# Two 8-expert mixtures: who scales and who adds the two expert outputs of every token at the end

## The chip, the cores and the metric

One core of a Trainium2 chip. The metric is the device time of one execution in microseconds (us), the median of several. Engines are named as in the profile: PE (TensorE), DVE (VectorE), ACT (ScalarE), POOL (GpSimd), SP (SyncE, which issues most DMAs).

## What is computed

2048 tokens of 128 values, in fp32, go through six stages, each with a residual: f0 (a 64-expert mixture), a0 (attention), g0 (the 64-expert mixture again), f1 (an 8-expert mixture), a1 (attention), g1 (the 8-expert mixture again). The change touches f1 and g1:

```python
probs = softmax(x @ Wg + bg)                       # x is layer-normed, 8 experts
h = relu(einsum('bsd,edf->bsef', x, W1) + b1)
all_out = einsum('bsef,efd->bsed', h, W2) + b2
top_vals, top_idx = top_k(probs, 2)
weights = top_vals / (sum(top_vals) + 1e-9)
out = sum(selected(all_out, top_idx) * weights)    # two outputs per token
x = x + 0.5 * out
```

## The kernel before, in words

`mixture_one` (L746) is built twice, as f1 and as g1. Tokens lie as 16 tiles of 128 in `core.x` (128 partitions, 16 tiles, 128 values). Every token's row is sent by GpSimd's indirect DMAs to the region of each of its two experts in DRAM, 39 tiles of 128 slots come back, and PE puts each through its expert. The outputs `y` go by an indirect DMA each (L902, `DMA_INDIRECT`, 39 of them, the last work of GpSimd in the stage) to `back_dram`, which is in the order of the tokens again.

The end of the stage, which the change rewrites, is this. SP waits until all 39 indirect DMAs have landed and reads `back_dram` into `back` (128 partitions, 16 tiles, K = 2 outputs, 128 values) in four quarters of four tiles each (L872, 512 KB a quarter, semaphores `back_loaded[q]`). Meanwhile DVE works out `weight` (L1211 to L1221), the factor of each output of each token, with the 0.5 in it. What is left is x += weight0 * back0 + weight1 * back1:

- Quarters 0 and 1: DVE alone, 8 instructions of 128x128 a quarter (L1228, `scalar_tensor_tensor`, multiply and add in one).
- Quarters 2 and 3: ACT scales both outputs in place, 8 instructions of 128x128 a quarter (L1039), and DVE adds them, 2 instructions of 128x512 a quarter (L1236).

The loop of DVE and the loop of ACT run over the quarters in order. `x_final` counts finished quarters. In g1, SP stores a quarter to the output when it is final (L877), and the program ends when the four stores have landed. In f1, nothing reads `x_final`; every engine drains and meets the others at `stage_end` (L3092), and then a1 starts, with DVE's layer norm of x (L675).

Three other places give rows for the prediction. In a0, GpSimd multiplies and adds tiles of 128x512 (L2063, L2067), and DVE subtracts 128x32 values, both operands in SBUF, by the helper `rest_part` (L732). In f0, GpSimd subtracts 128x512 by the same helper (L732), and DVE makes 128x1024 blocks with `tensor_scalar` from SBUF to SBUF (L1847, L1870). At the end of each stage GpSimd's queue has a drain (L3092).

Of the kernel before, what the change touches and what calls it, by code (L numbers as in the profile page):

```python
# [18 lines left out]
ALU = mybir.AluOpType  # L19
ACT = mybir.ActivationFunctionType  # L20
# [36 lines left out]
class Core:  # L57
# [11 lines left out]
    def sem(self, name):  # L69

        s = self.sem_ctx.enter_context(self.nc.semaphore(name))
        self.stage_sems.append(s)
        return s
# [12 lines left out]
class Front:  # L86


    K, ROW, REGION = 2, 132, TOKENS
# [656 lines left out]
def mixture_one(core, name, ctx, w):  # L746
# [9 lines left out]
    K = Front.K  # L756
# [37 lines left out]
    weight = sb("weight", [P, K, TILES])  # L794
# [9 lines left out]
    back = sb("back", [P, TILES, K, P])  # L804
# [4 lines left out]
    sem = lambda n: core.sem(f"{name}_{n}")  # L809
# [12 lines left out]
    fr.expect([wave_sent[v] for v, n in enumerate(halves_in) for _ in range(n)])  # L822
    w_loaded = sem("w_loaded")
    copied = sem("copied")
    back_scaled = sem("back_scaled")
    weight_ready = sem("weight_ready")
    x_loaded = [sem(f"x_loaded{i}") for i in range(len(GROUPS))]
# [7 lines left out]
    x_final = sem("x_final")  # L835
# [43 lines left out]
    def gpsimd(pool):  # L879
        if early:  # L880
            early.gpsimd(pool)
        fr.fill(pool)
        for g in range(fr.groups):
            fr.number(pool, g)
        pool.memset(lower[:, :, :], 1.0).then_inc(lower_filled, 1)
        pool.iota(fill[:, :], [[SLOTS, FULL]], base=0, channel_multiplier=0,
                  allow_small_or_imprecise_dtypes=True).then_inc(lower_ready, 1)
        pool.iota(tile_number[:, :], [[1, PASSES]], base=0, channel_multiplier=0,
                  allow_small_or_imprecise_dtypes=True).then_inc(lower_ready, 1)
        pool.memset(taken[:, E1:E1 + 1], 0.0).then_inc(lower_ready, 1)  # L890
        pool.wait_ge(lower_filled, 1)
        pool.affine_select(out=lower[:, :, :], in_=lower[:, :, :], compare_op=ALU.is_gt, fill=0.0,
                           base=0, pattern=[[1, E1], [-1, E1]], channel_multiplier=0).then_inc(lower_ready, 1)
        fr.fills.wait(pool)
        pool.wait_ge(fr.numbered, 2 * fr.groups)
        for g in range(fr.groups):
            pool.wait_ge(fr.slots_ready, g + 1)
            pool.wait_ge(fr.rows_doubled, g + 1)
            fr.scatter(pool, g)
        for i in range(PASSES):  # L900
            pool.wait_ge(y_ready, i + 1)
            pool.indirect_dma_start(back_dram[:, :],  # L902
                                    bass.IndirectOffsetOnAxis(ap=xin[:, i, P:P + 1].bitcast(I32), axis=0),
                                    y[i % YBUF][:, :], None, bounds_check=K * TOKENS - 1,
                                    oob_is_err=False).then_inc(y_sent[i % YBUF][0], 16)

    def tensor(pe):
        def turned(g):
# [85 lines left out]
    def scalar(act):  # L994
        def take(g):
            act.wait_ge(fr.turned, g + 1)
            if g:
                act.wait_ge(fr.logits_done, g)
            act.activation(fr.xnT[:, :], bank[g], ACT.Copy).then_inc(fr.xnT_ready, 1)

        fr.deviation(act, 0)
        take(0)
        fr.double(act, 0)
        fr.deviation(act, 1)
        take(1)
        fr.double(act, 1)
        for g in (2, 3):
            fr.normalise_by_shift(act, g)
            take(g)
            fr.double(act, g)  # L1010

        def xT_out(i):
            act.wait_ge(x_turned, i + 1)
            if i >= 2:
                act.wait_ge(h_done, i - 1)
            act.activation(xT[:, i % 2, :], bank[6 + i % 2][:, 0:SLOTS], ACT.Copy).then_inc(xT_ready, 1)  # L1016

        xT_out(0)
        xT_out(1)
        for i in range(PASSES):  # L1020
            if i >= 2:
                act.wait_ge(y_done, i - 1)
            act.wait_ge(h_done, i + 1)
            for c in range(FC1):
                act.activation(hT[:, i % 2, c, :], bank[i % 2][:, P * c:P * c + P], ACT.Relu,  # L1025
                               bias=wt[i % WBUF][:, B1 + c:B1 + c + 1]).then_inc(relu_done, 1)
            if i + 2 < PASSES:
                xT_out(i + 2)
            if early and 0 <= i - HIGH_AT < len(early.cuts):
                early.high(act, i - HIGH_AT)  # L1030
        act.wait_ge(shifted, 1)
        act.activation(ex[:, :, :], ex[:, :, :], ACT.Exp).then_inc(exp_done, 1)

        act.wait_ge(weight_ready, 1)
        for q in (2, 3):
            act.wait_ge(back_loaded[q], 16)
            for k in range(K):
                for t in range(4 * q, 4 * q + 4):
                    act.activation(back[:, t, k, :], back[:, t, k, :], ACT.Copy,  # L1039
                                   scale=weight[:, k, t:t + 1]).then_inc(back_scaled, 1)  # L1040

    def vector(dve):
        c_ = Chain(chain)

        def step(ins):
            dve.wait_ge(c_.sem, c_.on(ins))
# [174 lines left out]
            step(dve.tensor_reduce(weight[:, k, :], part[:, :, :], AX.X, ALU.add))  # L1221
        dve.sem_inc(weight_ready, 1)

        for q in range(2):
            dve.wait_ge(back_loaded[q], 16)
            for k in range(K):
                for t in range(4 * q, 4 * q + 4):
                    last = dve.scalar_tensor_tensor(core.x[:, t, :], back[:, t, k, :], weight[:, k, t:t + 1],  # L1228
                                                    core.x[:, t, :], ALU.mult, ALU.add)
                step(last)  # L1230
            dve.sem_inc(x_final, 1)
        for q in (2, 3):
            for k in range(K):
                dve.wait_ge(back_scaled, 4 * (K * (q - 2) + k + 1))
                xq = core.x[:, 4 * q:4 * q + 4, :]
                step(dve.tensor_tensor(xq, xq, back[:, 4 * q:4 * q + 4, k, :], ALU.add))  # L1236
            dve.sem_inc(x_final, 1)

    return dict(sync=sync, gpsimd=gpsimd, tensor=tensor, scalar=scalar, vector=vector)


# [1813 lines left out]
def build(nc, w, out, stages):  # L3055
# [87 lines left out]
STAGES = [  # L3143
    ("f0", mixture_zero), ("a0", attention_zero), ("g0", mixture_zero),
    ("f1", mixture_one), ("a1", attention_one), ("g1", mixture_one),
]

# [45 lines left out]
```

## Time and profile before

| what | us |
|---|---|
| runs | 993.63, 1002.97, 995.65 |
| median | 995.65 |
| the profiled execution | 1004.14 |
| its span | 1002.4 |
| busy: PE, DVE, ACT, POOL | 852.5, 721.0, 547.9, 299.4 |

The profiled execution's own time is 1.7 us longer than its span, and 8.5 us longer than the median. Busy time is that of all instructions of an engine. L12 is line 12 of the kernel. A duration is the time from an instruction's start to its end; consecutive instructions of DVE and ACT overlap a little, so a group's duration is shorter than the sum over its members. An entry in square brackets is the idle time ahead of an instruction and what ended it.

### The profile page before, as it was taken

The numbers are of one execution on the slowest core, as the hardware profiler recorded it, in microseconds if no ns is written. First come the engines' busy times: TensorE is split into PE (matmuls) and PEld (weight loads), VectorE is DVE, ScalarE is ACT, GpSimd is POOL, SyncE is SP. The second block draws the span as 40 slices with busy tenths as digits, with TensorE's granted clock in tenths as the row PEclk, the third lists the DMA queues.
The fourth block names the chain that finished last, engine by engine and source line by source line (L and its number), as shares of the span: only waits on it lengthen the run. The fifth ranks groups of instructions, "written<-read, shape, count | busy, mean of one in ns | idle before, by whom it ended". The sixth has DMA issues, their size and how long they took to land.

```text
span 1002.4 us, 23097 instructions
## 1 busy us (share of the span) xinstructions
PE 852.5 (85%) x7244; PEld 637.4 (64%) x7244; DVE 721.0 (72%) x2591; ACT 547.9 (55%) x1498; POOL 299.4 (30%) x423
## 2 busy tenths in 40 slices
PE   5899987899995899975999188999999998659992
PEld 4457854466553457754899165677767766548992
DVE  7757888457765866886867658877787788478665
ACT  4232043467775413113568338877887888435663
POOL 2033124743301001305777280001000000057772
PEclk9999996579998799995999679999999999959996
DMA  9208951111303503116362246544646462073314
GB/s 250 64 0 295 387 191 44 44 44 45 89 4 88 159 1 101 42 30 196 86 181 64 91 147 190 169 148 133 184 132 185 127 191 86 10 213 92 106 46 132
DMA packets 135459, 120.00 MB, mean 120 GB/s; under 512 B 11011, under 2 KB 115739, under 8 KB 135348
## 3 DMA queue, kind: packets, MB, share of 16 engines
q1 hardware_dynamic: 130804, 110.09, 36.6%
q0 software_dynamic: 4544, 8.54, 2.5%
q8 instruction: 56, 0.92, 0.4%
q14 instruction: 55, 0.45, 0.1%
HBM read 67.45 MB, written 51.80 MB: 119 GB/s over the span
## 4 chain that ended last, share of the span: by engine, by line
PE 60%; DVE 14%; ACT 13%; issue 5%; SPq 3%; DMA 3%; DVEq 1%; POOL 0%; POOLq 0%; ACTq 0%
PE psum L1613 6%; PE psum L1527 5%; PE psum L967 4%; PE psum L976 4%; PE psum L2277 4%; PE psum L2825 3%; ACT a_L L2955 3%; PE psum L2205 3%; ACT a_L L2953 3%; PE psum L2874 3%; PE psum L2861 2%; PE psum L741 2%; PE psum L1553 2%; ACT a_PT L2964 2%; PE psum L2169 2%
## 5 line engine op out<-in xcount | busy, mean ns | idle before, releaser
L2459 DVE TENSOR_REDUCE a_negmax<-psum 128x2 f32<-128x512 f32 x128 | 83.0, 686 | 43.4 <-PE psum L2205 40.3
L2405 ACT ACTIVATE a_PT<-psum 128x1024 f32<-128x1024 f32 x64 | 64.9, 1020 | 14.7 <-PE psum L2214 14.3
L2955 ACT ACTIVATE a_L<-a_L,a_least 128x256 f32<-128x256 f32 x128 | 63.3, 495 | 0.0
L2825 PE MATMUL psum<-a_KT,a_Q 64*128 64x128 f32 (+1 forms) x512 | 57.7, 342 | 3.4 <-DVE a_least L3015 1.4
L1025 ACT ACTIVATE g_hT<-psum,g_wt 128x128 f32<-128x128 f32 x156 | 44.5, 368 | 24.7 <-PE psum L967 24.7
L2953 ACT ACTIVATE a_L<-a_L,a_least 128x128 f32<-128x128 f32 x128 | 50.6, 395 | 10.7 <-DVE a_least L3015 9.8
L1025 ACT ACTIVATE f_hT<-psum,f_wt 128x128 f32<-128x128 f32 x156 | 44.5, 368 | 20.8 <-PE psum L967 20.8
L3013 DVE CUSTOM_DVE_ANT_0 a_L<-psum,a_X 128x128 f32<-128x128 f32 x128 | 36.6, 286 | 25.0 <-PE psum L2825 24.9
L3015 DVE CUSTOM_DVE_ANT_0 a_L<-psum,a_X 128x256 f32<-128x256 f32 x128 | 53.7, 420 | 0.0
L2964 ACT ACTIVATE a_PT<-psum 128x768 f32<-128x768 f32 x64 | 51.1, 799 | 1.7 <-PE psum L2841 0.9
L163 POOL MEMSET g_logit<- 128x128 f32 x1 | 0.2, 204 | 171.2 <-DVEq L3092 171.2
L2861 PE MATMUL psum<-a_PT,a_V 128*64 128x256 f32 (+1 forms) x512 | 50.0, 339 | 0.2 <-ACT a_xn L2974 0.2
L2841 PEld LDWEIGHTS psum<-ident,a_L 64*128 64x128 f32 x768 | 30.5, 139 | 30.7 <-ACT a_PT L2964 17.5
L2205 PE MATMUL psum<-a_turned 24*128 24x256 f32 x224 | 39.2, 365 | 10.3 <-ACT a_turned L2353 5.0
L902 POOL DMA_INDIRECT g_back_dram<-g_y,g_xin x39 | 43.8, 1123 | 12.4 <-DVE g_y L1134 6.6
L902 POOL DMA_INDIRECT f_back_dram<-f_y,f_xin x39 | 43.0, 1103 | 12.4 <-issue 6.7
L2861 PEld LDWEIGHTS psum<-a_PT,a_V 128*64 128x64 f32 x512 | 32.5, 139 | 20.1 <-issue 11.0
L2756 DVE TENSOR_SCALAR a_L<-a_L,a_rinv 128x256 f32<-128x256 f32 x128 | 44.5, 348 | 0.0
L967 PE MATMUL psum<-g_xT,g_wt 128*128 128x128 f32 x312 | 41.7, 277 | 0.7 <-ACT g_xT L1016 0.7
L967 PE MATMUL psum<-f_xT,f_wt 128*128 128x128 f32 x312 | 41.5, 276 | 0.8 <-ACT f_xT L1016 0.8
L2841 PE MATMUL psum<-ident,a_L 64*128 64x64 f32 x768 | 37.0, 229 | 5.6 <-ACT a_PT L2964 5.6
L976 PE MATMUL psum<-f_wt,f_hT 128*128 128x128 f32 x312 | 41.1, 275 | 0.0
(588 smaller groups left out, 2518.4 us busy)
## 6 DMA issues: line engine op xcount, KB each, us to landing
z<-a_G SPq DMA_DIRECT2D x32, 512.0 KB, 3.6
a_X<-z SPq DMA_DIRECT2D x16, 1024.0 KB, 6.6
f_slots_dram<-empty SPq DMA_DIRECT2D x1, 8910.0 KB, 29.7
g_slots_dram<-empty SPq DMA_DIRECT2D x1, 8910.0 KB, 52.3
a_X<-z SPq DMA_DIRECT2D x16, 512.0 KB, 4.0
f_wgu<-in_gate_up SPq DMA_DIRECT2D x16, 384.0 KB, 6.4
z<-pad SPq DMA_DIRECT2D x6, 1024.0 KB, 5.3
g_wgu<-in_gate_up SPq DMA_DIRECT2D x16, 384.0 KB, 6.2
```

The costliest lines, as they stand in the source:

```text
L902: pool.indirect_dma_start(back_dram[:, :], bass.IndirectOffsetOnAxis(ap=xin[:, i, P:P + 1].bitcast(I32), axis=0), y[i % YBUF][:, :], None, ...
L967: last = pe.matmul(bank[i % 2][:, P * c:P * c + P], wt[i % WBUF][:, P * c:P * c + P], xT[:, i % 2, :], start=True, stop=True)
L976: last = pe.matmul(bank[4 + i % 2][:, 0:P], hT[:, i % 2, c, :], wt[i % WBUF][:, OUT + P * c:OUT + P * c + P], start=(c == 0), stop=(c == F ...
L1025: act.activation(hT[:, i % 2, c, :], bank[i % 2][:, P * c:P * c + P], ACT.Relu, bias=wt[i % WBUF][:, B1 + c:B1 + c + 1]).then_inc(relu_don ...
L2205: last = pe.matmul(bank[h % 2][:, SEQ * t:SEQ * t + SEQ], q[rows, g, P * t:P * t + P].bitcast(F32R), k[rows, g, :].bitcast(F32R), start=Tr ...
L2459: dve.tensor_reduce(negmax[:, :, h], query_bank(b, h).rearrange("p (t n) -> p t n", n=SEQ), AX.X, ALU.max, negate=True).then_inc(max_done, 1)
L2825: last = pe.matmul(out, Q[rows, at, b % 2, queries], KT[rows, at, b % 2, keys], start=True, stop=True)
L2841: last = pe.transpose(bank[2 + r][:, at:at + HP], pr[rows, n % SLOTS, P * j:P * j + P], core.ident[rows, rows])
L2861: last = pe.matmul(o[D1 * i:D1 * i + D1, queries], V[s][:, kt, D1 * h:D1 * h + D1], PT[:, (2 * m + i) % TSLOTS, keys], start=(kt == 0), st ...
L2953: act.activation(pr[:, o, 0:P], L[:, o, 0:P], ACT.Exp, bias=least[:, o, 0:1], scale=-1.0, accum_out=sums[:, o, 0:1])
L2955: act.activation(pr[:, o, P:3 * P], L[:, o, P:3 * P], ACT.Exp, bias=least[:, o, 1:2], scale=-1.0, accum_out=sums[:, o, 1:2]).then_inc(p_re ...
L2964: act.activation(own.rearrange("p (k r c) -> p r k c", r=2, c=HP), core.psum[:, 2:4, 0:3 * P].rearrange("p r (k c) -> p r k c", c=HP), ACT ...
```

## The change

In every quarter ACT now scales only the second outputs (4 instructions instead of 8 in quarters 2 and 3, and 4 where there were none in quarters 0 and 1). DVE adds the first outputs with the multiply-and-add instruction in all four quarters. The scaled second outputs are added by GpSimd in quarters 0, 1 and 2, as one 128x512 instruction each, behind its last indirect DMA, and by DVE in quarter 3, when the other three are finished.

```diff
+    first_added = sem("first_added")
@@ gpsimd(pool), behind the 39 indirect DMAs
+        for q in range(3):
+            pool.wait_ge(first_added, 4 * (q + 1))
+            add_second(pool, q).then_inc(x_final, 1)
@@ scalar(act)
         act.wait_ge(weight_ready, 1)
-        for q in (2, 3):
+        for q in range(4):
             act.wait_ge(back_loaded[q], 16)
-            for k in range(K):
-                for t in range(4 * q, 4 * q + 4):
-                    act.activation(back[:, t, k, :], back[:, t, k, :], ACT.Copy,
-                                   scale=weight[:, k, t:t + 1]).then_inc(back_scaled, 1)
+            for t in range(4 * q, 4 * q + 4):
+                act.activation(back[:, t, 1, :], back[:, t, 1, :], ACT.Copy,
+                               scale=weight[:, 1, t:t + 1]).then_inc(back_scaled, 1)
+
+    def add_second(eng, q):
+        eng.wait_ge(back_scaled, 4 * (q + 1))
+        xq = core.x[:, 4 * q:4 * q + 4, :]
+        return eng.tensor_tensor(xq, xq, back[:, 4 * q:4 * q + 4, 1, :], ALU.add)
@@ vector(dve)
-        for q in range(2):
+        for q in range(4):
             dve.wait_ge(back_loaded[q], 16)
-            for k in range(K):
-                for t in range(4 * q, 4 * q + 4):
-                    last = dve.scalar_tensor_tensor(core.x[:, t, :], back[:, t, k, :], weight[:, k, t:t + 1],
-                                                    core.x[:, t, :], ALU.mult, ALU.add)
-                step(last)
-            dve.sem_inc(x_final, 1)
-        for q in (2, 3):
-            for k in range(K):
-                dve.wait_ge(back_scaled, 4 * (K * (q - 2) + k + 1))
-                xq = core.x[:, 4 * q:4 * q + 4, :]
-                step(dve.tensor_tensor(xq, xq, back[:, 4 * q:4 * q + 4, k, :], ALU.add))
-            dve.sem_inc(x_final, 1)
+            for t in range(4 * q, 4 * q + 4):
+                dve.scalar_tensor_tensor(core.x[:, t, :], back[:, t, 0, :], weight[:, 0, t:t + 1],
+                                         core.x[:, t, :], ALU.mult, ALU.add).then_inc(first_added, 1)
+        dve.wait_ge(first_added, 16)
+        dve.wait_ge(x_final, 3)
+        add_second(dve, 3).then_inc(x_final, 1)
+        dve.wait_ge(x_final, 4)
```

## Rows read from the trace of the kernel before

**Rows 1.** The page: chain of work that ended last, shares of the span
```profile
PE 60%; DVE 14%; ACT 13%; issue 5%; SPq 3%; DMA 3%; DVEq 1%; POOL 0%; POOLq 0%; ACTq 0%
```

**Rows 2.** The chain at the end of g1: start us, us, what
```profile
987.42 0.43 SPq L872
...
987.89 5.97 DMA g_back<-g_back_dram
...
995.81 2.93 ACT g_back L1039 x10
```

**Rows 3.** Timeline, end of g1: start us, us, engine, line, operation, times [idle before]
```profile
990.98 4.77 DVE L1228 SCALAR_TENSOR_TENSOR x<-g_back,g_weight,x 128x128 f32<-128x128 f32 x16 [2.76 <-DMA g_back<-g_back_dram]
993.95 4.78 ACT L1039 ACTIVATE g_back<-g_back,g_weight 128x128 f32<-128x128 f32 x16 [9.66 <-DMA g_back<-g_back_dram]
995.90 1.42 DVE L1236 TENSOR_TENSOR x<-x,g_back 128x512 f32<-128x512 f32 x2
...
998.83 0.69 DVE L1236 TENSOR_TENSOR x<-x,g_back 128x512 f32<-128x512 f32 x1 [0.55 <-ACT g_back L1039]
```

**Rows 4.** Timeline, end of f1 and start of a1
```profile
563.68 4.77 DVE L1228 SCALAR_TENSOR_TENSOR x<-f_back,f_weight,x 128x128 f32<-128x128 f32 x16 [2.72 <-DMA f_back<-f_back_dram]
566.36 4.78 ACT L1039 ACTIVATE f_back<-f_back,f_weight 128x128 f32<-128x128 f32 x16 [9.33 <-DMA f_back<-f_back_dram]
568.60 2.25 DVE L1236 TENSOR_TENSOR x<-x,f_back 128x512 f32<-128x512 f32 x3
571.25 0.69 DVE L1236 TENSOR_TENSOR x<-x,f_back 128x512 f32<-128x512 f32 x1 [0.39 <-ACT f_back L1039]
...
572.25 0.87 DVE L675 BATCH_NORM_STATS2 a_moments<-x 128x6 f32<-128x128 f32 x4 [0.31 <-DVEq L3092]
```

**Rows 5.** Tile g_back: its four DMAs from issue to landing
```profile
DMA to landing us min/median/max: 4.8/5.8/6.7
```

**Rows 6.** Line L877, g1's stores: duration ns min/median/max, first and last start
```profile
L877 SPq DMA_DIRECT2D out<-x x4: 372/380/393, 993.4 to 999.6; - x4
...
DMA to landing us min/median/max: 2.3/2.3/3.0
```

**Rows 7.** GpSimd's 128x512 arithmetic, lines L2063 and L732: ns min/median/max
```profile
L2063 POOL TENSOR_TENSOR a_z<-a_elu,ahead_cos x7: 1258/1272/1275, 147.5 to 253.9; 128x512 f32<-128x512 f32 x7
...
L732 POOL TENSOR_TENSOR f_ypart<-f_ys,f_ypart x8: 1262/1270/1730, 80.0 to 101.6; 128x512 fp32r<-128x512 f32 x8
```

**Rows 8.** A DVE subtraction beside a GpSimd addition in a0 (timeline; line L732)
```profile
159.65 1.31 POOL L2067 TENSOR_TENSOR a_z<-a_z,a_rot 128x512 f32<-128x512 f32 x1
...
159.87 1.14 DVE L732 TENSOR_TENSOR a_mparts<-a_negmax,a_mparts 128x32 fp32r<-128x32 f32 x1
...
L732 DVE TENSOR_TENSOR a_mparts<-a_negmax,a_mparts x8: 191/324/1144, 159.9 to 295.0; 128x32 fp32r<-128x32 f32 x8
```

**Rows 9.** DVE's SBUF-to-SBUF blocks beside GpSimd's subtractions in f0 (timeline; line L1847)
```profile
98.89 1.40 DVE L1847 TENSOR_SCALAR f_ST<-f_repl,f_own_token 128x1024 fp32r<-128x1024 f32 x2
...
100.81 2.88 DVE L1870 TENSOR_SCALAR f_ST<-f_repl,f_own_token 128x1024 fp32r<-128x1024 f32 x2
...
99.71 1.73 POOL L732 TENSOR_TENSOR f_ypart<-f_ys,f_ypart 128x512 fp32r<-128x512 f32 x1 [0.85 <-ACT f_ypart L1638]
...
101.63 1.50 POOL L732 TENSOR_TENSOR f_ypart<-f_ys,f_ypart 128x512 fp32r<-128x512 f32 x1 [0.19 <-ACT f_ypart L1638]
...
L1847 DVE TENSOR_SCALAR f_ST<-f_repl,f_own_token x4: 739/742/744, 93.7 to 99.5; 128x1024 fp32r<-128x1024 f32 x4
```

**Rows 10.** GpSimd's last indirect DMAs and its queue's drains, f1 and g1
```profile
557.44 1.08 POOL L902 DMA_INDIRECT f_back_dram<-f_y,f_xin  x1 [0.30 <-issue]
...
984.70 1.08 POOL L902 DMA_INDIRECT g_back_dram<-g_y,g_xin  x1 [0.30 <-issue]
...
L3092 POOLq DRAIN  x1: 7557/7557/7557, 556.8 to 556.8; - x1
...
L3092 POOLq DRAIN  x1: 7551/7551/7551, 984.1 to 984.1; - x1
```

## Prediction

> **What bounds the kernel now.** I first read the page's chain of the work that ended last, then the chain and the timeline of the two stretches that the change rewrites. The chain runs 60% through PE and 13% through ACT [rows 1], so nothing about the change can be read from busy shares; what counts is which wait ends last at the end of f1 and of g1, where PE has no work. In g1 the chain comes over the third quarter's DMA, 5.97 us long, lands at 993.86, goes through ACT's scaling [rows 2] and ends with DVE's last add. The reader is to see three things in the timeline. DVE starts at 990.98, when the first quarter lands, and spends 4.77 us on the 16 multiply-and-adds of quarters 0 and 1: one every 0.30 us. ACT starts only at 993.95, with quarter 2, and needs 4.78 us for its 16, to 998.73. DVE waits 0.55 us for it and ends at 998.83 + 0.69 = 999.52 [rows 3]. So from DVE's start to its end it is 8.54 us, and ACT, which idled 9.66 us before it, sets the end. In f1 it is the same: 563.68 to 571.94, 8.26 us [rows 4]. The fourth quarter landed near 995.1 in g1 (issued at about 988.4, one 0.48 us step behind the third at 987.89, and 6.7 us to landing), the second near 987.42 + 4.8 = 992.2 [rows 2, 5].
>
> Both stretches pass on what they win or lose. In f1, DVE's last add ends at 571.94, and the next stage's first instruction, on DVE, starts at 572.25 [rows 4]. In g1 the last store is issued at 999.6, right behind the last add, and lands 2.3 us later [rows 6].
>
> **The change, part by part.**
>
> ACT: 16 instructions before, 16 after. But they start with quarter 0's landing, and in each quarter 4 x 0.30 + 0.09 = 1.3 us follow a landing: 992.3, 993.5, 995.2 and 996.4 instead of an end at 998.73. ACT leaves the path. Nothing else is queued on it but the drain.
>
> DVE: 16 multiply-and-adds before, 16 after (4.77 us, now all on the first outputs); of its four 128x512 adds, 0.69 us each [rows 3], one is left. Its semaphore increments, one per instruction, I price at nothing: ACT's 16 carry one each at the same 0.30 us pace.
>
> GpSimd: three adds of 128x512. Alone such an instruction takes 1.27 us [rows 7]. Behind them in its queue is only the drain. Ahead of them are the indirect DMAs, the last of which ends at 985.8, and 558.5 in f1 [rows 10]: over 6 us before the first add is released.
>
> If the three engines only had to wait for one another's data, g1 would go like this. First add: both its inputs are there at 992.3, it runs to 993.6. Second: 993.7 to 994.9. Third: DVE's quarter 2 (landed 993.86) is done at 995.15, so 995.2 to 996.5. DVE's quarter 3 ends at 995.1 + 0.05 + 1.24 = 996.4, and its add runs 996.6 to 997.3. That is 2.2 us before 999.52. In f1, with the same offsets, also 2.2 us. Sum: 4.4 us won. This is the lower end of the price of the adds, nothing taken from DVE.
>
> But DVE and GpSimd do not run freely beside each other in this trace. At 159.65 GpSimd begins a 128x512 add. At 159.87 DVE begins a subtraction of 128x32 values whose two operands are in SBUF. Undisturbed it takes 191 ns; here it takes 1144 and ends at 161.01, 0.05 us behind GpSimd's add [rows 8]. Less its own 0.19 us it was held until 160.82, that is until 0.14 us before the other's end. The other seven of these subtractions were shorter because GpSimd ran nothing or something short. The new multiply-and-adds are of the same kind: `back` and `x`, both in SBUF. In the trace nearly all other arithmetic of DVE beside GpSimd's has an operand in PSUM.
>
> What one GpSimd add costs a row of back-to-back DVE instructions, I take from f0, where DVE makes 128x1024 blocks from SBUF to SBUF. Two of them with GpSimd idle at the handover take 1.40 us, one alone 0.74, so the step from one to the next is 0.66. Two others, with a GpSimd subtraction already running at the start of the first and another that gets in between, take 2.88. GpSimd's own times are 1.73 and 1.50 in place of 1.27, so it too was held, by 0.46 and 0.23 [rows 7, 9]. The 1.50 began at 101.63, was let in at 101.63 + 0.23 = 101.86, and ran to 103.13; the second DVE block ended at 100.81 + 2.88 = 103.69, so it began in earnest at 102.95. From 101.86 to 102.95 is 1.09 us. With the handovers overlapping a little, the first block, held by the running subtraction by 101.44 - 0.14 - 100.81 = 0.49, would have ended at 102.04; its successor ended 1.65 later instead of 0.66. So an add that gets between two DVE instructions costs DVE 1.0 to 1.1 us; I take 1.02. The other end is its full 1.27. It also shows that GpSimd is let in between two queued DVE instructions, so it isn't starved.
>
> Sum with this price. DVE's path is 16 multiply-and-adds, 4.77; three GpSimd adds between them, 3 x 1.02 = 3.06; the gap before the last add, 0.15 (995.90 less 995.75 [rows 3]); and the add, 0.69: 8.67 us. Are the waits for landings hidden? Quarter 1 starts at 992.2, when it lands; quarter 2 at 994.4, long after 993.86; quarter 3 at 996.7. The third add gets in behind the first instruction of quarter 3, near 996.9, and is done at 998.1, before DVE ends quarter 3 at 998.8. Against 8.54 in g1 that is +0.13, and against 8.26 in f1 +0.41: +0.5 us in all. With 1.27 an add it is 9.42 us, +0.9 and +1.2: +2.0.
>
> The Trainium skill, SBUF — State Buffer, section "Who interferes with whom", has the rule behind this: VectorE's second read interface is GpSimd's only one, a VectorE instruction with two SBUF inputs contends with a GpSimd instruction that reads SBUF, and the loser fully blocks instead of sharing. The 1144 ns row agrees. By that rule the result is the one just given; by data waits alone it is the 4.4 us of the first sum.
>
> So the forecast is 1004.14 + 0.5 = 1004.6 us for the profiled execution, and the same 0.5 us on the median of 995.65: 996.2. The stores of g1 don't alter it: quarter 2's is issued about 1.6 us before the last, and they took 2.3 us with a spacing of that order before.
>
> **Rivals.**
>
> A: no blocking for this pair of instructions, or little. For it: no row shows this very instruction beside a GpSimd add, and 128x32 may behave otherwise than 128x128. Against: three rows' worth of delay, in both directions [rows 8, 9]. Its time: 995.65 - 4.4 = 991.2. Partial blocking falls between, and breaks even at (8.54 - 4.77 - 0.84) / 3 = 0.98 us an add in g1 and 0.88 in f1.
>
> B, the other side, slower: GpSimd isn't ready for arithmetic. In both stages its queue's drain behind the last indirect DMA lasts 7.55 us, to 564.39 and 991.65. That is 5.87 us beyond the end of the last DMA instruction, 558.52 and 985.78 [rows 10]. If these 5.87 us run by themselves, they are over just before the first add is released (about 565.0 and 992.3). If they start only with the next instruction that GpSimd is given, the first add ends 5.87 us late: in g1 it begins at 998.2, when DVE has finished all its multiply-and-adds; three adds at 1.27 and two handovers make it 1002.1, DVE's add 1002.85, 3.3 us behind 999.52. In f1 570.9, 574.8 and 575.5, 3.6 us. Sum +6.9: 1002.5. It decides from a delay of the first add above some 2.5 us, below which the other engines' work covers it. For it: the delay is equal to 6 ns in both stages and no row explains it. Against: no row has GpSimd arithmetic right behind an indirect DMA, and going the other way, from arithmetic to the first indirect DMA, shows nothing like it.
>
> The Trainium skill, GPSIMD Engine Reference, section "Instruction dispatch", states that the first call to a freshly loaded kernel on GpSimd pays about 6 us without a visible instruction. The size resembles the 5.87 us; no row here shows a load.
>
> **How the numbers follow.** The blocking forecast gets 0.63, since the row in a0 is unambiguous; A 0.23; B 0.14. The range of the likeliest alone is 995.2 to 997.8 (the 1.0 and the 1.27 us prices). The range with 8 in 10 takes in A and what the runs scatter, and leaves B out: 990.5 to 1001.5. The three runs before spread over 9 us, and about 1% is what a measurement of this kernel can tell from no change; none of the three cases reaches that. Faster by over 1%: 0.04; within 1%: 0.89; slower by over 1%: 0.07, most of it from B.
>
> **What would show it.** In the profile after: multiply-and-adds of about 1.3 to 1.4 us, three in each stage, each beside a GpSimd add, and the group of 16 near 7.8 us instead of 4.77; GpSimd's adds at 1.3 to 1.6 us; DVE's last add ending 8.7 us after its first multiply-and-add. Right for A would be all 16 at 0.35 us and the end 6.3 us after the start. Right for B would be a gap, or a first add, of over 6 us. The forecast is wrong if ACT is on the chain again, or if the last add waits for GpSimd's third by more than 0.2 us.

## Result, and the profile after

The change makes the kernel slower: 1001.4 us median against 994.36 (20 runs each), a ratio of 1.0059 with a 95% interval of 1.0035 to 1.0083. That is +5.9 us, between +3.5 and +8.3 (the ratio takes in all the runs; the two medians alone are 7.0 apart). The forecast was +0.5.

The profiled execution after took 1000.14 us, with a span of 998.3. It happens to be shorter than that of before (1004.14), with a higher mean granted TensorE clock (0.913 of full speed against 0.903), so the two spans can't be compared. The time of a run goes with this clock: runs of the kernel before at 0.905 took 1002 to 1004 us, runs at 0.919 took 991 to 992. The stretches that the change touches can be compared: PE does nothing in them. All comparisons below go from DVE's first multiply-and-add (the first quarter has landed) to the next stage's first DVE instruction in f1, or to the end of the span in g1.

Timeline of the kernel after, end of f1 and start of a1, DVE and then GpSimd (L1235 is the multiply-and-add, L1048 the 128x512 add):

```profile
553.22 1.14 DVE L1235 SCALAR_TENSOR_TENSOR x<-f_back,f_weight,x 128x128 f32<-128x128 f32 x4 [2.79 <-DMA f_back<-f_back_dram]
554.52 6.26 DVE L1235 SCALAR_TENSOR_TENSOR x<-f_back,f_weight,x 128x128 f32<-128x128 f32 x12 [0.16 <-DMA f_back<-f_back_dram]
560.82 0.69 DVE L1048 TENSOR_TENSOR x<-x,f_back 128x512 f32<-128x512 f32 x1
566.11 0.87 DVE L675 BATCH_NORM_STATS2 a_moments<-x 128x6 f32<-128x128 f32 x4 [4.60 <-POOLq L3095]
...
558.80 1.31 POOL L1048 TENSOR_TENSOR x<-x,f_back 128x512 f32<-128x512 f32 x1 [0.75 <-ACT f_back L1042]
```

DVE's work takes 553.22 to 561.51, 8.29 us, as long as before (8.26 [rows 4]). But behind it DVE now idles 4.60 us where it idled 0.31, and what it waits for is POOLq L3095: the drain of GpSimd's queue at the end of the stage. Line L3095 of the kernel after, in f1 and then g1 (duration in ns, then the start):

```profile
L3095 POOLq DRAIN  x1: 7237/7237/7237, 558.8 to 558.8; - x1
...
L3095 SPq DRAIN  x1: 7/7/7, 995.6 to 995.6; - x1
...
L3095 POOLq DRAIN  x1: 7227/7227/7227, 990.6 to 990.6; - x1
```

In f1 it ends at 566.0, 5.9 us behind the end of GpSimd's last add (560.11). Before, it ended 5.87 us behind the last indirect DMA [rows 10], under cover of the landings. It takes the same time, but begins 12 us later, counted from DVE's first multiply-and-add: 6.9 us behind it instead of 5.2 ahead of it. From the first multiply-and-add to a1: 566.11 - 553.22 = 12.89 us against 8.57, +4.3.

In g1:

```profile
985.08 7.54 DVE L1235 SCALAR_TENSOR_TENSOR x<-g_back,g_weight,x 128x128 f32<-128x128 f32 x16 [2.70 <-DMA g_back<-g_back_dram]
...
990.64 1.30 POOL L1048 TENSOR_TENSOR x<-x,g_back 128x512 f32<-128x512 f32 x1 [0.76 <-DVE x L1235]
...
992.65 0.69 DVE L1048 TENSOR_TENSOR x<-x,g_back 128x512 f32<-128x512 f32 x1
```

DVE ends at 993.34, 8.26 us behind its start against 8.54 before [rows 3]. The last store is issued at 993.4 and lands 2.3 us later, at 995.7. SP's own drain stands at 995.6, but it doesn't wait for that landing: behind its last store SP clears 32 semaphores, from 993.8 on, and drains after them. GpSimd's drain ends only at 997.86, 5.92 us behind its last add. So the end of the span is 998.3 - 985.08 = 13.22 us behind the first multiply-and-add against 1002.4 - 990.98 = 11.42: +1.8. It is less than in f1 since behind DVE's end SP's store, its clears and the landing take 2.3 us in any case, and cover that much of the drain. Together +6.1 us, against the measured +5.9.

### The profile page after: what moved, and what is told of

Same layout as the page of the kernel before. It is cut to its first block, busy times and chain, and to the rows that moved or that the text cites. A ratio compares the mean times of both kernels' runs of the same rounds, so it can differ in the third digit from the quotient of the medians.

```text
span 998.3 us, 23094 instructions
## 1 busy us (share of the span) xinstructions
PE 839.4 (84%) x7244; PEld 630.3 (63%) x7244; DVE 723.0 (72%) x2585; ACT 548.0 (55%) x1498; POOL 305.9 (31%) x429
## 3 DMA queue, kind: packets, MB, share of 16 engines
q0 software_dynamic: 4544, 8.54, 2.5%
## 4 chain that ended last, share of the span: by engine, by line
PE 64%; DVE 18%; ACT 10%; issue 4%; DMA 2%; POOLq 1%; DVEq 1%; POOL 0%; SPq 0%; ACTq 0%
PE psum L971 7%; PE psum L980 7%; PE psum L1616 6%; PE psum L1530 5%; PE psum L2828 3%; PE psum L2280 3%; PE psum L2877 3%; PE psum L2208 3%; PE psum L2864 2%; ACT a_L L2958 2%; ACT a_L L2956 2%; PE psum L741 2%; PE psum L1556 2%; PE psum L2844 2%; DVE a_negmax L2462 2%
## 5 line engine op out<-in xcount | busy, mean ns | idle before, releaser
L2208 PE MATMUL psum<-a_turned 24*128 24x256 f32 x224 | 37.2, 347 | 10.8 <-DVE a_negmax L2462 5.3
L180 POOL DMA_INDIRECT f_slots_dram<-f_rows,f_slot x32 | 35.2, 1099 | 19.3 <-issue 16.9
```

The costliest lines, as they stand in the source:

```text
L2208: last = pe.matmul(bank[h % 2][:, SEQ * t:SEQ * t + SEQ], q[rows, g, P * t:P * t + P].bitcast(F32R), k[rows, g, :].bitcast(F32R), start=Tr ...
```

## The experiments

Every ratio is to runs of the kernel before that were taken beside it; their median is 995 us where no other is given.

**The drain moved.** The changed kernel with one more drain, ahead of the adds:

```diff
@@ gpsimd(pool), behind the 39 indirect DMAs
+        pool.drain()
         for q in range(3):
             pool.wait_ge(first_added, 4 * (q + 1))
```

> GpSimd gets one more drain, between its last indirect DMA and its three adds. Theory (the 5.9 us belong to the first drain behind indirect DMAs, whoever waits for it): this drain ends 5.87 us behind the last DMA instruction, before the first add is released, and the one at the end of the stage takes only what GpSimd's last add still needs, about 1.4 us. From DVE's first multiply-and-add to a1's first DVE instruction then 8.6 us in place of 12.9 (before the change 8.57); in g1 to the end of the span 11.1 in place of 13.2 (before 11.4). In all about 6 us less than the changed kernel, the time of the kernel before within 1 us. Rival (every drain in a stage with indirect DMAs takes 5.9 us): the second drain is as long as it was, time as the changed kernel, +6. Rival (it is the adds' and DVE's blocking that costs): as the changed kernel, +6.

The ratio to the kernel before is 1.002 (0.9986 to 1.0054). The new drains (L907) and those at the ends of f1 and g1 (L3096), here:

```profile
L907 POOLq DRAIN  x1: 7647/7647/7647, 546.3 to 546.3; - x1
...
L907 POOLq DRAIN  x1: 7554/7554/7554, 975.0 to 975.0; - x1
...
L3096 POOLq DRAIN  x1: 1404/1404/1404, 559.6 to 559.6; - x1
...
L3096 POOLq DRAIN  x1: 1406/1406/1406, 987.4 to 987.4; - x1
```

The first drain takes all of it, the one at the stage's end only what the last add still needs (1.40 us in f1, 1.41 in g1). The first multiply-and-add starts at 554.09 and a1 at 562.57: 8.48 us; in g1 981.87 to 993.0, 11.1 us. In the stretches the drain is the whole loss; all else in the change is worth -0.1 and -0.3 us. The ratio leaves room for that and for more: it says +2.0 us on the kernel before, between -1.4 and +5.4, and its interval overlaps that of the changed kernel. So it is the stretches that decide here.

**The drain late, without the change.** The kernel before, in which nothing moves but the start of the drain:

```diff
@@ gpsimd(pool) of the kernel before, behind the 39 indirect DMAs
+        pool.wait_ge(x_final, 4)
```

> The kernel before, no adds on GpSimd; its queue only waits for x_final 4 between its last indirect DMA and the drain. Theory: the drain's 5.9 us start when DVE has finished: f1 to a1's start 8.3 + 5.9 + 0.1 = 14.3 us in place of 8.57, g1 to the end of the span 8.5 + 5.9 + 0.5 = 14.9 in place of 11.4; in all +9 us on the kernel before. Rival (the 5.9 us run by themselves behind the last DMA, and what costs in the changed kernel is the adds): no change.

Ratio 1.0085 (1.0047 to 1.0124), some +8.5 us, with no arithmetic added to any engine. Timeline and drain line:

```profile
563.36 4.78 DVE L1229 SCALAR_TENSOR_TENSOR x<-f_back,f_weight,x 128x128 f32<-128x128 f32 x16 [2.85 <-DMA f_back<-f_back_dram]
...
577.60 0.87 DVE L675 BATCH_NORM_STATS2 a_moments<-x 128x6 f32<-128x128 f32 x4 [6.07 <-POOLq L3093]
...
L3093 POOLq DRAIN  x1: 5868/5868/5868, 571.6 to 571.6; - x1
```

With GpSimd idle for 13 us ahead of it, the drain still takes 5.87 us from its own start. So the time doesn't run by itself behind the DMAs: it waits for the drain. 14.2 us from the first multiply-and-add to a1, 14.6 to the end (994.72 to 1009.3), as expected.

**Without that drain.** Does the next instruction of GpSimd pay instead?

```diff
@@ stage_end(eng, n) of the changed kernel
-            eng.drain().then_inc(stage_done, 1)
+            if names[n] in ("f1", "g1") and eng is nc.gpsimd:
+                eng.sem_inc(stage_done, 1)
+            else:
+                eng.drain().then_inc(stage_done, 1)
```

> The changed kernel without GpSimd's drain at the ends of f1 and g1 (it only increments the semaphore). Theory (the time is the drain's own): f1 to a1's start 8.6 us, g1 to the end of the span 11.1, unless the drain at the end of the program (41 ns so far) takes the 5.9 us over in g1; a1's first GpSimd instructions are as long as they were. In all -6 us to the changed kernel, or -4.3 if the program's last drain takes it over. Rival (the next instruction of GpSimd pays, whatever it is, when some condition holds): a1's first GpSimd instruction (0.53 us) or the gap behind it is 5.9 us longer, and a1's start is delayed where PE waits for GpSimd's first parts.

Ratio 1.0046 (1.0011 to 1.0081). In f1, 555.53 to 564.25, 8.7 us: the 4.3 us are back, and a1's first GpSimd instructions are as before (the memset 0.52 us, the cast 0.40). The 5.9 us are not gone, though. The next drain of GpSimd, at the end of a1 (here L3098, in the kernel after L3095), takes them over, with all of a1's arithmetic on GpSimd between; first the kernel after, then this run:

```profile
L3095 POOLq DRAIN  x1: 1514/1514/1514, 695.3 to 695.3; - x1
...
L3098 POOLq DRAIN  x1: 7342/7342/7342, 693.1 to 693.1; - x1
```

That is 5.83 us more, and it costs nothing, since GpSimd has no work until the start of g1, over 160 us later. And at the end of the program, where every engine drains once more:

```profile
L3059 POOLq DRAIN  x1: 5857/5857/5857, 995.2 to 995.2; - x1
```

In the kernel after it lasts 41 ns. Here it begins at 995.2, right behind SP's drain at the end of g1 (SP's semaphore clears end at 995.0), and nothing covers it: 984.53 to 1001.3, 16.8 us. So the expectation for g1 was too kind: I had put its loss equal to that of the kernel after, but the program's last drain starts only when all engines have met, and that costs 3.6 us more. -4.2 and +3.6 make this kernel about as slow as the changed one. The time is owed until some drain takes it; arithmetic and memset neither take it nor are slower for it.

**What it is made of.** The kernel before, with a drain behind the sends of each group of 8 indirect DMAs:

```diff
@@ gpsimd(pool) of the kernel before
             fr.scatter(pool, g)
+            pool.drain()
```

> The kernel before with a drain of GpSimd behind the first stage's sends of each of the four groups (8 indirect DMAs each), besides the one at the end of the stage (39 more). It tells what the 5.9 us are made of. If they are a fixed price of the first drain behind any indirect DMA: all five drains of a stage last at least 5.8 us beyond the last DMA instruction, and the sends are later by some 20 us in each stage. If they grow with the number of indirect DMAs since the drain before: the first four about 8/71 of 5.87 = 0.7 us each, and the last 39/71, 3.2 us. If they belong to the second kind of indirect DMA alone: the first four are below 1 us and the last is 5.87.

A single run: 1011.2 us. The stage-end drain in f1, and the DMA instruction before it:

```profile
558.48 0.97 POOL L903 DMA_INDIRECT f_back_dram<-f_y,f_xin  x1 [0.30 <-issue]
...
L3093 POOLq DRAIN  x1: 6289/6289/6289, 556.4 to 556.4; - x1
```

It ends 3.24 us behind the last DMA instruction, and 3.24 us in g1 too. That is 39 x 0.083. In the kernel before, 71 DMAs lie ahead of the drain, and 5.87 / 71 = 0.083. So the two drains fit 0.083 us for each indirect DMA since the drain before. All these DMAs carry 128 rows each, so no run tells a price per DMA from one per row; nor does one show what the drain does in that time. Behind 8 of them that would be 0.66 us, but the eight drains behind the groups (four in each stage) end 1.7 to 2.3 us behind the last DMA instruction, so something with a floor of that size is in it too. That it is the landing of the last DMA, 2.1 us at the least after its start, is a guess that no run tested. The run is 16 us above the median of the kernel before. In its trace GpSimd's engine idles 2.5 to 3.1 us behind each of the eight groups instead of 0.3, 19 us in all, which is enough for it.

**The blocking.** Adds left out (the second outputs of quarters 0 to 2 are missing from the sum), and adds all behind the multiply-and-adds; both with the early drain:

```diff
@@ left out
-            add_second(pool, q).then_inc(x_final, 1)
+            pool.sem_inc(x_final, 1)
@@ late
-            pool.wait_ge(first_added, 4 * (q + 1))
+            pool.wait_ge(first_added, 16)
```

> As the run with the early drain, but GpSimd only increments x_final where it added: the second outputs of quarters 0 to 2 are missing from the sum. Theory (a multiply-and-add of DVE is blocked for the length of a GpSimd add): without adds no multiply-and-add is longer than 0.35 us, the 16 are bound by the landings alone (the fourth lands 4.1 us behind the first, plus 1.25), and DVE's last add ends 6.2 us after the first multiply-and-add, in place of 8.2: 2 us less in each stage. Rival (DVE's multiply-and-adds are slow for another reason, such as ACT writing the same tile or the DMAs landing): they stay at 1.35 us three times a stage and the end stays at 8.2.

> As the run with the early drain, but each of GpSimd's three adds waits for all 16 multiply-and-adds, so none of them runs beside a GpSimd add. Theory (blocking): the 16 take 5.4 us, all at 0.35; GpSimd's adds are 1.27 each, 3.9 together; DVE's add follows: 10.1 us from first to last against 8.2 with the adds between, that is 1.9 later. Rival (another reason for the 1.35 us ones): they stay in the group of 16, which then takes 7.5 us and the end comes at 12.2.

Tile g_back: DVE's multiply-and-adds of the kernel after, with durations in ns as min/median/max:

```profile
L1235 DVE SCALAR_TENSOR_TENSOR x<-g_back,g_weight,x x16: 339/342/1367, 985.1 to 992.3; 128x128 f32<-128x128 f32 x16
```

without adds on GpSimd:

```profile
L1236 DVE SCALAR_TENSOR_TENSOR x<-g_back,g_weight,x x16: 342/346/352, 977.8 to 982.3; 128x128 f32<-128x128 f32 x16
```

and with the adds late:

```profile
L1236 DVE SCALAR_TENSOR_TENSOR x<-g_back,g_weight,x x16: 343/346/352, 983.8 to 988.5; 128x128 f32<-128x128 f32 x16
L1049 POOL TENSOR_TENSOR x<-x,g_back x3: 1259/1259/1262, 989.0 to 991.4; 128x512 f32<-128x512 f32 x3
```

The long multiply-and-adds are there only where a GpSimd add runs beside them. In g1 DVE ends 5.9 us (977.78 to 983.65) behind its start without adds, 8.27 with them between, and 9.6 with them behind (983.82 to 993.44; expected 10.1, but the 16 took 5.1 and not 5.4, and three adds in a row 3.70 and not 3.9). Put between, GpSimd's adds cost 2.4 us, put behind 3.7 (in f1 2.1 and 3.6): blocking spoils most of the overlap, not all. Single runs, 988.31 and 998.24 us.

**DVE alone, and one add on GpSimd.** The changed kernel with no adds on GpSimd; and one with the early drain and GpSimd's add of quarter 0 alone:

```diff
@@ vector(dve); GpSimd's adds are taken out
             for t in range(4 * q, 4 * q + 4):
                 dve.scalar_tensor_tensor(...).then_inc(first_added, 1)
+            if q:
+                dve.wait_ge(first_added, 4 * q)
+                add_second(dve, q - 1).then_inc(x_final, 1)
         dve.wait_ge(first_added, 16)
-        dve.wait_ge(x_final, 3)
         add_second(dve, 3).then_inc(x_final, 1)
@@ one add: besides, in gpsimd(pool); DVE's adds from q > 1 on, each behind wait_ge(x_final, q - 1)
+        pool.drain()
+        pool.wait_ge(first_added, 4)
+        add_second(pool, 0).then_inc(x_final, 1)
```

> The changed kernel with all four adds on DVE, each behind the multiply-and-adds of the next quarter, and none on GpSimd, whose drain is early again. DVE: 16 multiply-and-adds 4.77 + 4 adds of 0.69 = 7.5, plus handovers some 0.3: 7.8 us from first to last against 8.26 in the changed kernel, 8.54 (g1) and 8.26 (f1) before. f1 to a1's start 8.2, g1 to the end of the span 10.7. Theory: 6.5 to 7 us less than the changed kernel, 0.5 to 1 us less than the kernel before. Rival (the division between ACT and DVE is at fault, not GpSimd): as the changed kernel.

> Early drain, GpSimd adds quarter 0 alone, DVE adds quarters 1 to 3, each behind the next quarter's multiply-and-adds. An add on GpSimd costs DVE 1.0 us by blocking, an add on DVE 0.65. Theory: 6.94 us from first to last with all four on DVE, so 7.3 here in each stage, and time 0.5 to 1 us above the version with all adds on DVE (not to be told apart in the medians, only in the stretches). Rival (the adds between are free where DVE waits for a landing anyway): 6.5 us or less, below that version.

> The version with all four adds on DVE once more, to narrow its interval: 0.9977 with 0.9943 to 1.0011 the first time. By the stretches of its profile it should be 1.4 us shorter than the kernel before in each of the two stages, a ratio of 0.9972. If the first ratio was chance, the stretches would still be shorter (7.15 us from f1's first multiply-and-add to a1, 10.0 from g1's to the end) and the ratio near 1.

All adds on DVE: ratio 0.9977 (0.9943 to 1.0011) at first, and 0.9957 (0.9925 to 0.9988) when run again, beside a kernel before of 1045.48 us: in that series both ran some 5% slower, the clock at 0.89 instead of 0.91. The stretches came again as they were, 7.16 us in f1 and 9.9 in g1. Timeline of the first, end of f1:

```profile
558.86 1.13 DVE L1232 SCALAR_TENSOR_TENSOR x<-f_back,f_weight,x 128x128 f32<-128x128 f32 x4
559.91 1.28 DVE L1045 TENSOR_TENSOR x<-x,f_back 128x512 f32<-128x512 f32 x2
561.40 0.87 DVE L675 BATCH_NORM_STATS2 a_moments<-x 128x6 f32<-128x128 f32 x4 [0.21 <-DVEq L3094]
```

From 554.25 to 561.40 it is 7.15 us against 8.57 before, and in g1 979.74 to 989.7, 10.0 against 11.42. DVE is never blocked, adds follow the multiply-and-adds with a step of 0.6 us, and GpSimd's drain is done long before. In the stretches this version beats the kernel before by 2.8 us and the changed one by 9. The ratio agrees, though only the second series is clear of 1. Expected were 7.8 us for DVE's work; it was 6.94, since neighbouring instructions overlap. One add on GpSimd gives 7.35 us in f1 and 7.34 in g1 (977.82 to 985.16), 0.4 more, as expected, and a ratio of 0.9969 (0.9937 to 1.0001): the medians don't tell these two versions apart, the stretches do.

## Why the prediction was right and wrong

- **That the time stays within 1% and leans up: right, by luck. The reason: wrong.** The +0.5 us from blocking is not what was measured. Without the drain's move the change gives 8.48 and 11.1 us for the two stretches, 0.1 and 0.3 us less than before, and the other 6 us are the drain. It is luck that they stay below 1%, some 10 us.
- **The step that failed** is "Behind them in its queue is only the drain", in the part on GpSimd, which priced that drain at nothing. The row was on the table: 7.55 us in f1 and g1 [rows 10]. I asked whether the 5.87 us run by themselves or start with the next instruction, and drew only the conclusion for the first add. The question of where the drain itself ends when it is queued behind the adds wasn't asked: the third add, "done at 998.1" in g1, plus 5.87 is 1004.0, 1.6 us behind the old end of the span. In f1, with the same offset, the drain would have ended 13.0 us behind the first multiply-and-add, where a1 started at 8.57. Together +6.0 us from the prediction's own times; measured in the stretches were +1.8 and +4.3.
- **Rival B** came nearest in size (+6.9), and its condition was half right: the 5.87 us do wait for an instruction of GpSimd. But that instruction is the drain, not the add. The first add began 6.6 us after GpSimd's engine fell idle, when its inputs were there, and took 1.26 us. By B, DVE would have idled ahead of its last add; the trace has it idle behind it. One of my signs for B, a gap of over 6 us ahead of the first add, was no sign: the prediction itself had over 6 us there for want of inputs.
- **The rule beside it** fell with it. The 6 us that the Trainium skill, GPSIMD Engine Reference, section "Instruction dispatch", gives for the first call of a freshly loaded kernel are one price. Here it was 3.24 us behind 39 DMAs and 5.87 behind 71, and no call of arithmetic paid it.
- **The blocking forecast, and Rival A.** The longest multiply-and-add of each stage took 1.35 to 1.38 us in every run with GpSimd adds beside them, as forecast, and 16 took 7.54 where "near 7.8" was said. An add between two of them costs (7.54 - 4.77) / 3 = 0.92 us, where I took 1.02 from f0's blocks. (Against the run with the adds late, where DVE also waits a little for landings, it is (7.54 - 5.06) / 3 = 0.83.) The gap ahead of the last add is 0.03 instead of 0.15. Hence 8.26 us and not 8.67. That is why the change without the drain is a little better than before and not a little worse. Rival A is refuted by the adds left out and the adds late, a single run each but the same in both stages. The blocking is as the Trainium skill, SBUF — State Buffer, section "Who interferes with whom", states it for an instruction with two SBUF inputs, and GpSimd was let in between two queued DVE instructions each time.
- **ACT leaves the path:** right. Its last scaling starts at 989.8 in g1 and ends at 990.2, 3 us before DVE.
- **The range** just held the time, by 0.1 us, but nothing in it stood for the drain: its upper end was set by how the runs scatter. The likeliest case's own range, 995.2 to 997.8, didn't hold it.

## What to carry over

When work is appended to an engine's queue, read what stands behind it as closely as what stands ahead: a drain or a barrier that was hidden starts only when the appended work is done. A long record on a queue that nobody waits for is a price that waits to be paid. And an add on GpSimd beside DVE instructions with two SBUF operands costs DVE more (0.92 us) than doing the add itself (0.69); one add moved to GpSimd made the stretch 0.4 us longer. So on this end of the stage GpSimd has nothing to give, even with its drain out of the way.

## What was not expected of the hardware

GpSimd's drain takes 0.083 us for each indirect DMA issued since its last drain: 5.87 us behind 71, 3.24 behind 39, from the time when the drain can start, however long GpSimd was idle before. Behind 8 it was 1.7 to 2.3 us, more than this price gives. Arithmetic and a memset in between don't start it and aren't slowed by it. If the stage's own drain is left out, the next one takes it over, 130 us later at the end of a1 (7.34 instead of 1.51 us) or at the end of the program (5.86 instead of 0.04 us). A drain put where GpSimd idles for another reason takes it off the path, at no cost in the two stretches.
